# Half's turns one by one in slot 28, a written-out end with residuals added on TensorE

## The chip, the cores and the metric

The kernel runs on one core of a Trainium2 chip. The metric is the device time of one execution in microseconds, the median of several runs. The profile is one execution taken by the hardware profiler; its times count from the span's start.

## The reference, cut to what matters

A two-layer decoder over x of shape (8, 128, 512). The change touches the last two of its six blocks, cross-attention with grouped queries and a routed low-rank layer, each followed by residual and LayerNorm:

```python
q = (query @ Wq + bq).reshape(B, L, NKV, G, HDIM)          # 8 key heads x 4 queries x 128
k_, v_ = jnp.split(kv @ Wkv + bkv, 2, axis=-1)
scores = jnp.einsum('blkgd,bmkd->bkglm', q, k) * scale
attn = jax.nn.softmax(scores, axis=-1)
o = jnp.einsum('bkglm,bmkd->blkgd', attn, v).reshape(B, L, NHEAD * HDIM)
x = layernorm(x + o @ Wo + bo)

logits = jnp.einsum('bsd,ed->bse', x, route_w)             # 8 experts
topk_v, topk_idx = jax.lax.top_k(logits, 1)
route_weight = one_hot(topk_idx[..., 0], E) * topk_v
h = jnp.einsum('bsd,erd->bser', x, A)                      # rank 16
out = jnp.einsum('bser,eor->bso', route_weight[..., None] * h, Bw)
x = layernorm(x + out)
```

## The kernel before, in words

All engines have one straight program each, and meet by counting semaphores. The batch of 8 blocks of 128 tokens is worked in two halves of HB = 4 blocks. The attention is a chain of *slots*: slot s is key head `s // 4 % 8` with block `s % 4` of half `s // 32`; `v = s // HB` numbers head and half together. Slots 0 to 31 are the first half, 32 to 63 the second. float32 products are made of three products of split operands (`mm3`, L547 to L549: high with high, high with low, low with high); ScalarE writes the high part, and GpSimd (weights, L1407) or VectorE (activations) the rest.

In slot s TensorE does, in this order: the scores of slot s into bank 1 (L982); one query product of the next head into bank 0 (`query`, twelve products); the transposes of the probabilities of slot s-1 into bank 2 (L1001, `ident` from `prm`); the values weighed by the probabilities of s-2 into bank 3; and the output product of s-4, twelve products that accumulate over the eight heads in bank 4 + block. VectorE does `soft_a` (maximum L2040, subtraction L2043), `soft_b` (sum L2049, reciprocal, multiply L2053), `turned_rest_p` (L2059, the rest of the transposed probabilities of s-1) and `o_rest` (L2066, the rest of the output of s-2). ScalarE does the exponential, `query_out`, two high parts of weights (`split_q`, `split_o`), the high part of the transposed probabilities and of the values' output, and a value's high part. GpSimd does the rests of a query weight, an output weight and a value.

Slot 28 is the one in which the second half's tokens are first needed, transposed and split: `turn_half(1, i, bank)` makes four transposes of a block (L914, two records each), `turned_half` reads them on ScalarE into the high part of `xs` (`x_split`), `x_rest` (L2029) writes the rest. Before, all four blocks are turned between scores and query product, in banks 2 and 0 by turns:

```python
if s == (NKV - 1) * HB:
    for i in range(HB):
        if i == 0:
            pe.wait_ge(S.p_rest, s - 1)
        turn_half(1, i, (2, 0)[i % 2])
query(v + 1, b)
```

A block's LayerNorm after the attention (`ln_a(4, b)`, `ln_b(4, b)`): VectorE adds the bank to the token block in `x_tok`, to which GpSimd added the bias before (L1652), takes the statistics (L1654, L1655), adds epsilon (L1656); GpSimd raises it to -0.5 (`rstd`, L1391); VectorE subtracts and multiplies (L1660). Then follows the routed layer in four steps: four transposes of the block (L948), eight records of a product with `ra_sb`, 128 columns of A and 8 of logits (L957), the transpose of the weighed part `wh` (L962), and the product with `bw_sb` (L965, one float32 product, two records). Between, VectorE's `route(b)` copies the 8 logits out of PSUM (L2073), takes their maximum (MAX8, L2074), the index, a mask, and multiplies (L2080). Then comes a last LayerNorm, stage 5, and the store of the block from SyncE's queue.

For the first half these steps are put one per slot into slots 40 to 55 (`routed_at`, `ROUTED_FROM`). For the second half the loop runs on to 72 slots: the slots after 63 hold the last steps of the attention and a pipeline of the four routed steps. There VectorE works stage 4 of a block, then `route` of an earlier one, then `ln_a(5)` and `ln_b(5)` of one before that.

## Time and profile before

| What | us |
|---|---|
| median of 3 runs (lowest, highest) | 1334.72 (1332.58, 1335.19) |
| the profiled execution, its own time | 1333.96 |
| its span | 1332.2 |
| TensorE busy, share of the span | 1236.0, 93% |
| VectorE busy | 968.5, 73% |
| ScalarE busy | 748.2, 56% |
| GpSimd busy | 674.8, 51% |

The attention's slots run from about 811 to 1310, the rest is what comes before and the routed end. In the names of the profile PE is TensorE (PEld its weight loads), DVE VectorE, ACT ScalarE, POOL GpSimd, SP SyncE. All of ScalarE's instructions have the line L1035, that of a helper, so they are told by their tiles. The matmul records are pipelined: one's end lies after the next one's start. The idle time in brackets is that of the engine ahead of the instruction, with what ended it. PEclk is the clock that TensorE was granted, 1.00 for 2.4 GHz, 0.50 for 1.2 GHz.

### The profile page before, as it was taken

How to read it: one execution, taken by the hardware profiler on the slowest of the kernel's cores; microseconds unless marked ns; L12 is line 12 of the kernel's file. 1: busy time of each engine (PE TensorE's matmuls, PEld its weight loads, DVE VectorE, ACT ScalarE, POOL GpSimd, SP SyncE). 2: the span in 40 equal slices, each digit the busy share in tenths (PEclk: the TensorE clock that was granted, in tenths of full speed). 3: DMA queues.
4: the chain of work that ended last, by engine and by line, in shares of the span. 5: the costliest groups of instructions: out<-in, count | busy, mean ns of one | idle time of the engine just before them, and what ended most of it. 6: DMA issues, size and time to landing. Idle time of an engine off the chain costs nothing.

```text
span 1332.2 us, 18653 instructions
## 1 busy us (share of the span) xinstructions
PE 1236.0 (93%) x6464; PEld 925.4 (69%) x6464; DVE 968.5 (73%) x1770; ACT 748.2 (56%) x1478; POOL 674.8 (51%) x535
## 2 busy tenths in 40 slices
PE   6997899999998988998998999999998999999995
PEld 5876677767777764444565547888887888888874
DVE  4785798999999997898657766655554675666676
ACT  5479898989998983332133235544544445444441
POOL 4128988888988870222842126443433543333331
PEclk9999899999999999999999999999998999999999
DMA  6003200122220015002300103222221221111110
GB/s 182 12 26 139 75 25 25 35 93 88 88 72 1 1 56 136 16 9 85 144 9 16 40 24 103 80 73 71 68 75 48 80 79 65 63 64 64 48 48 32
DMA packets 37213, 81.92 MB, mean 61 GB/s; under 512 B 3808, under 2 KB 8160, under 8 KB 35200
## 3 DMA queue, kind: packets, MB, share of 16 engines
q1 hardware_dynamic: 37120, 80.72, 18.5%
q8 instruction: 53, 0.87, 0.3%
q14 instruction: 40, 0.33, 0.1%
HBM read 74.35 MB, written 6.36 MB: 61 GB/s over the span
## 4 chain that ended last, share of the span: by engine, by line
PE 68%; DVE 19%; ACT 6%; issue 5%; POOL 1%; DMA 1%; SPq 1%; DVEq 0%; POOLq 0%; ACTq 0%
PE psum L547 10%; PE psum L549 10%; PE psum L548 10%; PE psum L622 7%; PE psum L636 6%; PE psum L982 4%; DVE arena L1747 4%; PE psum L660 3%; PE psum L647 3%; ACT arena L1035 3%; PE psum L747 2%; PE psum L1001 2%; PE psum L731 1%; DVE lnst L1654 1%; PE psum L871 1%
## 5 line engine op out<-in xcount | busy, mean ns | idle before, releaser
L1471 POOL TENSOR_TENSOR arena<-arena 128x1024 f32<-128x1024 f32 x128 | 300.4, 2370 | 42.7 <-DVE arena L1747 42.5
L1407 POOL TENSOR_TENSOR w_split<-arena,w_split 128x512 fp32r<-128x512 f32 x128 | 168.1, 1333 | 280.3 <-ACT w_split L1035 280.3
L1747 DVE TENSOR_TENSOR_SCAN arena<-psum,arena 128x512 f32<-128x512 f32 x256 | 292.3, 1204 | 15.2 <-ACT psum L1035 15.2
L622 PEld LDWEIGHTS psum<-prm,arena 128*128 128x128 f32 x1024 | 118.7, 142 | 110.3 <-issue 61.8
L1035 ACT ACTIVATE psum<-arena,amat 128x508 f32<-128x508 f32 x256 | 173.3, 709 | 30.4 <-DVE arena L1747 29.4
L622 PE MATMUL psum<-prm,arena 128*128 128x128 f32 x1024 | 148.9, 280 | 38.4 <-DVE arena L1747 34.7
L1035 ACT ACTIVATE arena<-psum,ssmC 128x256 f32<-128x256 f32 x448 | 177.5, 484 | 10.8 <-PE psum L622 10.7
L1035 ACT ACTIVATE arena<-arena 128x512 f32<-128x512 f32 (+2 forms) x86 | 62.8, 734 | 210.1 <-DVE arena L2043 209.1
L1035 ACT ACTIVATE arena<-psum,prm 128x512 f32<-128x512 f32 (+1 forms) x130 | 91.1, 708 | 148.6 <-PE psum L549 70.0
L636 PE MATMUL psum<-prm,arena 128*128 128x128 f32 x1024 | 134.1, 273 | 0.1
L636 PEld LDWEIGHTS psum<-prm,arena 128*128 128x128 f32 x1024 | 117.0, 141 | 0.4 <-ACT arena L1035 0.3
L547 PE MATMUL psum<-x_split,w_split 128*128 128x512 f32 x256 | 106.3, 415 | 2.9 <-DVE x_split L2029 2.8
L1035 ACT ACTIVATE arena<-psum 128x512 f32<-128x512 f32 (+4 forms) x108 | 57.8, 563 | 82.7 <-PE psum L739 33.3
L1391 POOL TENSOR_TENSOR lnrs<-lnve,halfneg 128x1 f32<-128x1 f32 x48 | 28.4, 591 | 143.3 <-DVE lnve L1656 143.3
L549 PE MATMUL psum<-x_split,w_split 128*128 128x512 f32 x256 | 100.9, 394 | 0.0
L548 PE MATMUL psum<-x_split,w_split 128*128 128x512 f32 x256 | 100.8, 394 | 0.0
L547 PE MATMUL psum<-w_split,o_split 128*128 128x512 f32 x256 | 100.7, 394 | 0.0
L549 PE MATMUL psum<-w_split,o_split 128*128 128x512 f32 x256 | 100.1, 391 | 0.0
L548 PE MATMUL psum<-w_split,o_split 128*128 128x512 f32 x256 | 99.6, 389 | 0.0
L2040 DVE TENSOR_REDUCE amax<-psum 128x4 f32<-128x512 f32 x64 | 44.1, 688 | 52.4 <-PE psum L982 52.4
L2059 DVE TENSOR_TENSOR ssmT<-psum,p_split 128x512 fp32r<-128x512 f32 x64 | 44.2, 691 | 51.5 <-ACT p_split L1035 51.4
L2049 DVE TENSOR_REDUCE asum<-arena 128x4 f32<-128x512 f32 x64 | 43.9, 686 | 44.0 <-ACT arena L1035 44.0
(230 smaller groups left out, 2544.0 us busy)
## 6 DMA issues: line engine op xcount, KB each, us to landing
arena<-wq SPq DMA_DIRECT2D x64, 256.0 KB, 2.6
arena<-wo SPq DMA_DIRECT2D x64, 256.0 KB, 2.8
arena<-bc_scratch SPq DMA_DIRECT2D x8, 1024.0 KB, 5.2
arena<-win SPq DMA_DIRECT2D x16, 256.0 KB, 2.7
v_keep<-row SPq DMA_DIRECT2D x16, 256.0 KB, 2.1
arena<-v_keep SPq DMA_DIRECT2D x1, 4096.0 KB, 12.8
arena<-xT SPq DMA_DIRECT2D x8, 256.0 KB, 5.5
x_tok<-wv SPq DMA_DIRECT2D x1, 2048.0 KB, 7.7
```

What stands on the lines that cost most here:

```text
L547: mm(o, l[0], r[0], start=start, stop=False)
L548: mm(o, l[0], r[1], start=False, stop=False)
L549: return mm(o, l[1], r[0], start=False, stop=stop)
L622: last = nc.tensor.transpose(hT[:, c, b % 2, e, :], hst[:, (2 * k + e) % 4, b * L:(b + 1) * L], ident)
L636: last = mm(bank[6 + e][:, b * L:(b + 1) * L], hTs[:, k % 2, b, e, :], ident, start=(n == 0 and b == 0), stop=(n == NS - 1 and b == HB - 1 ...
L982: last = mm(bank[1][:, j * P:(j + 1) * P], qT[:, v % 2, j, b * L:(b + 1) * L], KT[:, v % NKV, gb * L:(gb + 1) * L], start=True, stop=True)
L1035: return nc.scalar.activation(o, i, f, **k)
L1407: gp.tensor_tensor(out_, whole, hi.bitcast(F32), ALU.subtract).then_inc(done, 1)
L1471: gp.tensor_tensor(bu[:, i % 4, :, :], dtu[:, (2 * j + e) % 4, :].unsqueeze(1).to_broadcast([P, NG, HT]), Brep[:, q * NG:(q + 1) * NG, :], ...
L1747: v.tensor_tensor_scan(hst[:, i % 4, :], decay_bank(i), bu[:, (k // NG * 2 + e) % 4, k % NG, :], 0.0, ALU.mult, ALU.add).then_inc(S.scan_d ...
L2040: link(v.tensor_reduce(amax[:, :], ps, AX.X, ALU.max))
L2059: v.tensor_tensor(p_lo[:, r % 2, :], bank[2][:, :], p_hi[:, r % 2, :].bitcast(F32), ALU.subtract).then_inc(S.p_rest, 1)
```

## The change

Four things. (1) In slot 28 the four blocks are turned one at a time through bank 0: the first after the scores, the other three between the four parts of the output product of slot 24; each waits until `x_rest` of the one before is done (`x4_lo`). The query product of the slot goes to the end, and on the other engines what belongs to it moves behind. (2) The loop ends with slot 63, and the end is written out: TensorE's last output products come one after the other with a single turn between them, the four routings stand in an order of their own with logits in banks 2 and 1 by turns. In slots 60 to 63 (`DRAIN`) ScalarE makes the transposed probabilities' high part ahead of the exponential and the output weight's high part late, and VectorE takes the probabilities' rest between the subtraction and the sum. (3) The residual of the second half is added by TensorE: after the output product of slots 56 to 59 it multiplies `ident` with the token block, in float32, into the same bank, so that stage 4's LayerNorm of these blocks reads PSUM and has no addition. Stage 5 of block 4 lies between the routings, the others behind them. (4) `route` searches the logits where they lie in PSUM, without the copy.

```diff
@@ tensor
             def turn_half(h, b, bk):
                 gb = h * HB + b
                 pe.wait_ge(S.x_done, lnc(3, gb))
-                if b >= 2:
+                if h and b:
+                    pe.wait_ge(S.x4_lo, gb)
+                elif b >= 2:
                     pe.wait_ge(S.x4_lo, gb - 1)
...
+            def logits_of(b):
+                pe.wait_ge(S.ra_in, 32)
+                pe.wait_ge(S.xT_sb, 2 * B + b + 1)
+                if b > HB:
+                    pe.wait_ge(S.r_wh, b - 1)
+                elif b >= 1:
+                    pe.wait_ge(S.r_wh, b)
+                for k in range(KD):
+                    last = mm(route_at(b), x5T[:, b % 2, k, :], ra_sb[:, k, :], start=(k == 0), stop=(k == KD - 1))
+                last.then_inc(S.r_ps, 1)
...
+            def attn_out(r):
+                rv, rb = r // HB, r % HB
+                pe.wait_ge(S.o_sb, r + 1)
+                if rv == NKV:
+                    pe.wait_ge(S.x_sum, lnc(4, rb))
+                for j in range(GQ):
+                    pe.wait_ge(S.wo_lo, rv * GQ + j + 1)
+                    last = mm3(bank[4 + rb][:, :], [osp[:, e, r % 3, j * P:(j + 1) * P] for e in range(2)],
+                               [wos[:, e, (rv * GQ + j) % 8, :] for e in range(2)],
+                               start=(rv % NKV == 0 and j == 0), stop=(rv % NKV == NKV - 1 and j == GQ - 1))
+                    if j == GQ - 1:
+                        last.then_inc(S.op_ps, 1)
+                    elif r == TURNING - 4:
+                        turn_half(1, j + 1, 0)
+                if rv == NU - 2:
+                    pe.wait_ge(S.xbias, 2 * B + HB + rb + 1)
+                    mm(bank[4 + rb][:, :], ident, x_tok[:, HB + rb, :], start=False, stop=False)
...
-                    if s == (NKV - 1) * HB:
-
-                        for i in range(HB):
-                            if i == 0:
-                                pe.wait_ge(S.p_rest, s - 1)
-                            turn_half(1, i, (2, 0)[i % 2])
-                    query(v + 1, b)
+                    if s == TURNING:
+                        turn_half(1, 0, 0)
+                    else:
+                        query(v + 1, b)
+                if s >= 1:
+                    turn_probs(s)
+                if s >= 2:
+                    weigh_values(s - 2)
+                if s >= 4:
+                    attn_out(s - 4)
+                if s == TURNING:
+                    query(v + 1, b)
...
+            turn_probs(SLOTS)
+            weigh_values(SLOTS - 2)
+            attn_out(SLOTS - 4)
+            weigh_values(SLOTS - 1)
+            attn_out(SLOTS - 3)
+            attn_out(SLOTS - 2)
+            turn_routed(HB, 0)
+            attn_out(SLOTS - 1)
+            pe.wait_ge(S.p_rest, SLOTS)
+            logits_of(HB)
+            turn_routed(HB + 1, 3)
+            turn_routed(HB + 2, 0)
+            logits_of(HB + 1)
+            turn_wh(HB, 3)
+            routed_out(HB, 4)
+            pe.wait_ge(S.xT_sb, 2 * B + HB + 3)
+            turn_routed(HB + 3, 0)
+            logits_of(HB + 2)
+            turn_wh(HB + 1, 3)
+            logits_of(HB + 3)
+            routed_out(HB + 1, 5)
+            turn_wh(HB + 2, 3)
+            routed_out(HB + 2, 6)
+            turn_wh(HB + 3, 3)
+            routed_out(HB + 3, 7)
@@ scalar
+                if s >= DRAIN:
+                    probs_high(s - 1)
+                act.wait_ge(S.p_es, s + 1)
+                av(pe_[:, s % 2, :], pe_[:, s % 2, :], ACT.Exp, scale=SQ).then_inc(S.p_exp, 1)
+                if s == TURNING:
+                    turned_half(1, 0, 0)
+                    probs_high(s - 1)
+                    turned_half(1, 1, 0)
+                    outs_high(s - 2)
+                    turned_half(1, 2, 0)
+                    split_o(s)
+                    turned_half(1, 3, 0)
+                elif s < DRAIN:
                     query_out(v + 1, b)
...
+                if s >= DRAIN:
+                    split_o(s)
                 value_high(s)
+                if s == TURNING:
+                    query_out(v + 1, b)
+                    split_q((v + 1) * GQ + b + 3)
@@ gpsimd
-                    rest_q(s + 7)
+                    if s != TURNING:
+                        rest_q(s + 7)
...
+                    if s == TURNING:
+                        rest_q(s + 7)
...
+            for stage in (4, 5):
+                for b in range(HB, B):
+                    rstd(pool, stage, b)
@@ vector
-                link(v.tensor_copy(logits, bank[2][:, P:P + 8]))
-                link(v.max(rt8, logits))
-                link(v.max_index(ri8[:, :], rt8, logits))
+                link(v.max(rt8, route_at(b)[:, P:P + 8]))
+                link(v.max_index(ri8[:, :], rt8, route_at(b)[:, P:P + 8]))
...
+            def attn_ln_a(b):
+
+                dve.wait_ge(S.op_ps, NU * HB - B + b + 1)
+                link(v.bn_stats(lnst[:, b, :], bank[b][:, :]))
+                link(v.bn_aggr(lnmv[:, b, :], lnst[:, b, :]))
+                v.tensor_scalar(lnve[:, b:b + 1], lnmv[:, b, 1:2], 1e-5, None, ALU.add).then_inc(S.ln_ve, 1)
...
+                soft_a(s)
+                if s == TURNING:
+                    x_rest(1, 0, 0)
                     turned_rest_p(s - 1)
+                    x_rest(1, 1, 0)
                     o_rest(s - 2)
+                    x_rest(1, 2, 0)
+                    x_rest(1, 3, 0)
+                if s >= DRAIN:
+                    turned_rest_p(s - 1)
+                soft_b(s)
...
+            turned_rest_p(SLOTS - 1)
+            o_rest(SLOTS - 2)
+            attn_ln_a(HB)
+            o_rest(SLOTS - 1)
+            attn_ln_b(HB)
+            for b in range(HB + 1, B):
+                attn_ln_a(b)
+                attn_ln_b(b)
+            route(HB)
+            route(HB + 1)
+            routed_ln_a(HB)
+            route(HB + 2)
+            ln_b(5, HB)
+            route(HB + 3)
+            for b in range(HB + 1, B):
+                routed_ln_a(b)
+                if b > HB + 1:
+                    ln_b(5, b - 1)
+            ln_b(5, B - 1)
```

## Rows read from the trace of the kernel before

**Rows 1.** Busy by stretch: length; PE, PEld, DVE, ACT, POOL; PEclk, DMA share, GB/s.

```profile
1003.15:1010.65 7.50, 7.50 (x41) 6.35 (x41) 4.29 (x7) 3.62 (x7) 2.94 (x4) 1.00 0.23 71
1010.65:1027.00 16.35, 12.34 (x57) 9.84 (x57) 6.87 (x11) 5.79 (x11) 2.97 (x4) 0.79 0.10 31
1018.00:1022.50 4.50, 4.50 (x11) 3.53 (x12) 0.66 (x2) 0.00 (x0) 0.00 (x0) 0.50 0.00 0
1312.00:1320.00 8.00, 4.42 (x27) 2.77 (x26) 6.15 (x24) 1.52 (x4) 1.10 (x2) 1.00 0.09 33
```

**Rows 2.** Timeline of slot 28: start, length, engine, line, tiles; idle time before it.

```profile
1010.49 1.05 PE L982 MATMUL psum<-arena 128*128 128x128 f32 x8
...
1011.37 1.04 PE L914 MATMUL psum<-prm,x_tok 128*128 128x128 f32 x8
...
1013.56 1.06 ACT L1035 ACTIVATE x_split<-psum 128x512 fp32r<-128x512 f32 x2
...
1014.17 1.29 DVE L2029 TENSOR_TENSOR x_split<-psum,x_split 128x512 fp32r<-128x512 f32 x2 [1.18 <-ACT x_split L1035]
...
1015.01 1.53 PE L914 MATMUL psum<-prm,x_tok 128*128 128x128 f32 x8 [2.60 <-DVE x_split L2029]
...
1017.95 0.80 PE L547 MATMUL psum<-x_split,w_split 128*128 128x512 f32 x1 [1.41 <-DVE x_split L2029]
```

**Rows 3.** Timeline of slots 62 and 63, VectorE and GpSimd.

```profile
1285.94 0.69 DVE L2049 TENSOR_REDUCE asum<-arena 128x4 f32<-128x512 f32 x1 [0.70 <-ACT arena L1035]
...
1286.51 1.29 POOL L1407 TENSOR_TENSOR w_split<-arena,w_split 128x512 fp32r<-128x512 f32 x1 [3.53 <-ACT w_split L1035]
...
1286.88 1.47 DVE L2053 TENSOR_TENSOR arena<-arena,ainv 128x512 f32<-128x512 f32 x1
...
1292.56 1.47 DVE L2053 TENSOR_TENSOR arena<-arena,ainv 128x512 f32<-128x512 f32 x1
```

**Rows 4.** TensorE's timeline from slot 60 to its last attention product.

```profile
1271.37 1.05 PE L982 MATMUL psum<-arena 128*128 128x128 f32 x8
...
1276.14 1.05 PE L982 MATMUL psum<-arena 128*128 128x128 f32 x8
...
1294.78 0.63 PE L1001 MATMUL psum<-prm,arena 128*128 128x128 f32 x4 [1.35 <-DVE ssmT L2059]
...
1302.94 0.63 PE L948 MATMUL psum<-prm,x_tok 128*128 128x128 f32 x4 [0.39 <-DVE o_split L2066]
...
1306.18 1.09 PE L957 MATMUL psum<-arena 128*128 128x136 f32 x8
...
1307.46 0.48 PE L547 MATMUL psum<-w_split,o_split 128*128 128x512 f32 x1
...
1310.08 0.39 PE L549 MATMUL psum<-w_split,o_split 128*128 128x512 f32 x1
```

**Rows 5.** The last blocks: timelines of VectorE and TensorE.

```profile
1322.57 0.17 DVE L2074 MAX8 arena<-arena 128x8 f32<-128x8 f32 x1
...
1323.58 0.29 DVE L2080 TENSOR_TENSOR arena<-psum,arena 128x128 f32<-128x128 f32 x1
...
1323.79 0.68 DVE L1652 TENSOR_TENSOR x_tok<-x_tok,psum 128x512 f32<-128x512 f32 x1
...
1324.62 1.12 PE L965 MATMUL psum<-arena 128*128 128x512 f32 x2 [0.37 <-ACT arena L1035]
...
1325.45 0.15 DVE L1656 TENSOR_SCALAR lnve<-lnmv 128x1 f32<-128x1 f32 x1
...
1326.27 0.55 DVE L1660 TENSOR_SCALAR x_tok<-x_tok,lnmv,lnrs 128x512 f32<-128x512 f32 x1 [0.66 <-POOL lnrs L1391]
...
1329.20 0.55 DVE L1660 TENSOR_SCALAR x_tok<-x_tok,lnmv,lnrs 128x512 f32<-128x512 f32 x1 [0.66 <-POOL lnrs L1391]
```

**Rows 6.** Chain of waits, slot 43: start, length, engine, tile, line.

```profile
1141.47 0.87 PE psum L965 x2
```

**Rows 7.** GpSimd's timeline, earlier network stage: a power beside VectorE's second half.

```profile
789.28 0.77 POOL L1391 TENSOR_TENSOR lnrs<-lnve,halfneg 128x1 f32<-128x1 f32 x1 [1.41 <-DVE lnve L1656]
```

More of the change, by code:

```diff
@@ L421, in routed_at, with route_at @@
                 return [(at // 4, at % 4, 2)]
-            at = s - (2 * NKV * HB + 1)
-            return [(HB + at - k, k, ((at % 2), 2, 3, 4 + at - k)[k]) for k in (3, 2, 1, 0) if 0 <= at - k < HB]
-        SLOTS = 2 * NKV * HB + 8
+            return []
+        def route_at(b):
+            return bank[1 if b > HB and b % 2 else 2][:, 0:136]
+        SLOTS = 2 * NKV * HB
+        DRAIN = SLOTS - HB
         @block.sync
@@ new lines, in turn_routed @@
+            def turn_routed(b, bk):
+                pe.wait_ge(S.x_done, lnc(4, b))
+                if b >= 2:
+                    pe.wait_ge(S.xT_sb, 2 * B + b - 1)
+                for k in range(KD):
+                    last = nc.tensor.transpose(bank[bk][:, k * P:(k + 1) * P], x_tok[:, b, k * P:(k + 1) * P], ident)
+                last.then_inc(S.xTt, 1)
+            def logits_of(b):
[5 more added lines that the diff above has]
+                    pe.wait_ge(S.r_wh, b)
+                for k in range(KD):
+                    last = mm(route_at(b), x5T[:, b % 2, k, :], ra_sb[:, k, :], start=(k == 0), stop=(k == KD - 1))
+                last.then_inc(S.r_ps, 1)
@@ new lines, in turn_wh, with routed_out, turn_probs @@
+            def turn_wh(b, bk):
+                pe.wait_ge(S.r_wh, b + 1)
+                if b > HB:
+                    pe.wait_ge(S.whT_done, b)
+                nc.tensor.transpose(bank[bk][:, 0:P], wh, ident).then_inc(S.wh_ps, 1)
+            def routed_out(b, bk):
+                pe.wait_ge(S.whT_done, b + 1)
+                mm(bank[bk][:, :], whT, bw_sb, start=True, stop=True).then_inc(S.rf_ps, 1)
+            def turn_probs(s):
+                pe.wait_ge(S.p_norm, s)
+                if s >= 2:
+                    pe.wait_ge(S.p_rest, s - 1)
+                for rb, step, bk in routed_at(s - 1):
+                    pe.wait_ge((S.xT_sb, S.r_wh, S.whT_done, S.x_sum)[step],
+                               (2 * B + rb + 1, rb + 1, rb + 1, lnc(5, rb))[step])
+                for j in range(GQ):
+                    last = nc.tensor.transpose(bank[2][:, j * P:(j + 1) * P], pn[:, j * P:(j + 1) * P], ident)
+                last.then_inc(S.t_ps, 1)
@@ new lines, in _ @@
+                if s >= 2:
+                    weigh_values(s - 2)
+                if s >= 4:
+                    attn_out(s - 4)
+                if s == TURNING:
+                    query(v + 1, b)
+                for rb, step, bk in routed_at(s):
+                    pe.wait_ge(S.p_rest, s)
+                    if step == 0:
+                        turn_routed(rb, bk)
+                    elif step == 1:
+                        logits_of(rb)
+                    elif step == 2:
+                        turn_wh(rb, bk)
+                    else:
+                        routed_out(rb, bk)
```

185 lines of the change are left out of this document (71 added, 114 removed).

## The prediction

> **What bounds the kernel now.** I read the busy time by stretch first, then the timelines of three places that the diff touches, one engine at a time, and last the chain of waits over the end. In a plain slot of the attention TensorE is busy for all of 7.50 us at the full clock, with VectorE at 4.29 and ScalarE at 3.62 [rows 1]. So whatever the change does for VectorE in slots 0 to 59 is free, and worth nothing, unless TensorE waits for it. Three places are different.
>
> *Slot 28* lasts 16.35 us, from 1010.65 to 1027.00 [rows 1], 8.85 more than a plain one. Four batches of transposes belong in it; eight of them (two batches) take 1.04 [rows 2], so four batches are some 1.8 us of work. The rest is waiting and clock. After the first two batches TensorE stands idle for 2.60, after the next two for 1.41 [rows 2]: both banks are full, and ScalarE and VectorE empty them only after the slot's maximum, subtraction and exponential. After the idle 2.60 the granted clock is 0.50 (1.2 GHz) until about 1022.5 [rows 1].
>
> *Slots 60 to 63* have no query products left, and VectorE sets their length: in the chain of waits its normalising multiply comes back every 5.68 us, at 1286.88 and 1292.56 [rows 3]. TensorE alone needs only 4.77 for such a slot (1271.37 to 1276.14, without a wait) [rows 4]. VectorE loses 0.70 per slot waiting for the exponential, and its multiply takes 1.47, because GpSimd's subtraction started at 1286.51 and ended at 1287.80, 0.9 after the multiply began [rows 3].
>
> *The end.* TensorE finishes the last attention product at 1310.08+0.39 = 1310.47 [rows 4]; call that moment V. From V to the end of the last normalisation, 1329.20+0.55 = 1329.75 [rows 5], VectorE has almost all the work, with a wait for GpSimd's power in each LayerNorm.
>
> **The change, part by part.**
>
> *Slot 28.* The batches now go through bank 0 one at a time, with other work between, and the query product goes last. I lay it out on the old times. Scores as before; batch 0 follows, done about 1012.0. TensorE goes on with the probabilities' transposes, the value product and the first of the four output products, to about 1013.7: work that before came behind the queries. ScalarE reads batch 0 at 1013.56 as before, VectorE has its rest from 1014.17 on, and the next batch starts at 1015.01, as it did [rows 2]: stall 1.3. From there each round is: 0.6 until the transposes are visible, 0.6 on ScalarE, 0.7 on VectorE, 0.15 to restart, some 2.1 (1015.0, 1017.1, 1019.2, 1021.3), with 0.45 of transposes and 0.7 of output product inside, so a stall of 0.9 to 1.0 each. The query product starts at 1021.3 rather than at 1017.95 [rows 2]. But it then runs in 2.8 at full clock, where before it took 5 us and left 4.2 of other work behind it; slot 29 starts at 1024.1 instead of 1027.0: 2.9 us saved. GpSimd's rest of the next query weight now comes last in its slot, after the query product (visible at 1024.3) and two ScalarE copies, at about 1025.6, inside slot 29; that weight is for slot 31, and the load that it releases in SyncE's queue (with the output weight queued behind) is needed from slot 30 on: hidden.
>
> *Clock in slot 28.* That sum wants the clock kept. The old fall stands behind 4.35 us in which TensorE was busy 1.76, one gap of 2.60. The new slot has no gap over 1.3. From 1312 to 1320 TensorE is busy only 4.42 of 8 us, broken up by waits, and the granted clock is 1.00 [rows 1]; the new slot from 1011.4 to 1021.3 is busy about 5.8 of 9.9, the same share. I take the full clock, and keep a low one as a rival.
> The Trainium skill, "TensorE: Matmul & The Clock Gate", PE-mode transpose, says that transposes don't count as activity for the clock; by that rule the new stretch is poorer than its busy share says, the clock falls, and the slot gains next to nothing (the second case below). No row here separates transposes from products.
>
> *Slots 60 to 63.* VectorE takes the probabilities' rest during the exponential, so 0.6 of its 5.68 goes, and GpSimd's subtraction comes later in the slot, so the multiply may be back near 0.7. VectorE needs 4.2 to 5.0. But TensorE gets a float32 identity product of 128x512 per slot, which takes 0.87 (two records) [rows 6]: 4.77+0.87 = 5.64. TensorE becomes the bound at practically the old period. Four slots from 1271.37 give 1293.9 for the transposes of slot 64, with switching and VectorE's last multiply 1294.1, against 1294.78 [rows 4]: 0.7 saved. Bounds for the identity product: 0.6 if part is hidden, and 1.12, as the last such product reads [rows 5], which would cost 1.0 over four slots.
>
> *From slot 64 to V.* Before, 15.69 (1294.78 to 1310.47). Out of it go the first logits and one batch of transposes, now issued after V (1306.18 to 1307.46, 1.28 [rows 4]), and the wait before 1302.94 (0.39 shown, 0.54 with the restart), because the awaited LayerNorm ends near 1301.2 without its addition. The rest stays: 13.9. V comes at 1308.0: 2.5 earlier in all.
>
> *From V on.* Before 19.28. A LayerNorm's first half is 1.81 (addition to the end of the epsilon, 1323.79 to 1325.60); its addition is 0.72 of that (0.68 and the hand-over); its second half starts 0.67 after, and takes 0.55; a routing without its copy takes 1.30 (MAX8 at 1322.57 to 1323.87); from there the transposed weight, ScalarE's copy and the output product need 1.87 (to 1325.74) [rows 5]. VectorE's instructions that need no result of the last one start 0.08 early. The attention LayerNorms of the other three blocks end before V (the third near V-0.9). The new order: last attention LayerNorm 0.04+1.09+0.67+0.68 (it reads PSUM; 0.68 is what the addition that reads PSUM takes), routing 4 1.22, gives V+3.70; routing 5 hides behind the 1.87, and the first half of output 4 ends at V+3.70+1.87+0.04+1.81 = V+7.42. Routing 6, second half 4, routing 7: 1.22+0.46+1.22, V+10.32. First halves 5 and 6, second half 5, first half 7: 1.72+1.73+0.47+1.72, V+15.96. The last power is issued just as VectorE runs a second half, and there GpSimd's power reads 0.77 instead of 0.55 [rows 7], so 0.89 rather than 0.67, then 0.55: V+17.40. Saved: 1.9.
> GpSimd's delay is what the Trainium skill, "SBUF — State Buffer", Who interferes with whom, describes as a port held for a whole instruction; by it the last multiply of slot 63 could go either way, 0.3 for the sum. The 0.77 agrees.
> If reading PSUM cost `max` and the index search more, they have no row here; a reduction over 512 columns of SBUF takes 0.69 and an addition that reads as many of PSUM 0.68 [rows 3, 5], so I take nothing, with 0.4 as the bound. The same copy in slots 41, 45, 49 and 53 lies beside a full TensorE: 0.
>
> *The last store* starts when its block is done; before that took 1332.2-1329.75 = 2.45. Now three blocks finish within 3.2 us and their transfers may overlap: +0.2 (bounds 0 and 1.2).
>
> **Sum.** -2.9 -0.7 -1.8 -1.9 +0.2 = -7.1. The profiled execution took 1333.96 (span 1332.2), so 1326.9. The median of the runs is 0.76 above that execution; I add half: 1327.3. What can't be told from no change is about 0.2%, 2.7 us.
>
> **The rivals.**
> 1. *Forecast*, 1325.0 to 1328.8 by the bounds: chance 0.62.
> 2. *The clock falls in slot 28 all the same*, because the new slot is broken up four times. At 0.50 a product is issued every 0.43 instead of 0.23; twelve of the query lose 2.4. Gain of the slot 0.3, time 1329.9. For it: a busy share under 0.6 for 10 us, in the slot where the clock fell before; against: the full clock at 1312 to 1320. Chance 0.20.
> 3. *The end gives less*: identity products at 1.12 and transfers at their bound, or an order in which VectorE waits for ScalarE's copy, which now waits for TensorE's transposes of the same slot. 1.0+1.0 less: 1329.3 to 1330. For it: VectorE's queue in slots 60 to 63 is strung to TensorE's twice. Against: a margin of 0.7 to 1.4 per slot. Chance 0.09.
> 4. *Nothing gained*: slot 28 ends no earlier and slots 60 to 63 are as in 3, within 2.7 of before. Chance 0.05.
> 5. *Slower*: the clock falls early in slot 28 and stays through the next slots, as products of 0.43 stretch them. A us at the low clock costs about 0.47 of a full TensorE. To eat the 4.2 of the end and pass 0.2% it must cost 6.9 more than the old fall did (about 2.7: eleven products at 0.2 more, and eight transposes in 1.53 instead of 1.04): some 20 us low instead of 7.4. Time 1337.5 or more. Against: at 1018 to 1022.5 TensorE was full at the low clock and got the high one back. Chance 0.04.
>
> Range for 8 in 10: 1324.4 to 1330.6, case 1 and 2 and most of 3. Chances: faster by over 0.2% 0.91, within 0.05, slower 0.04.
>
> **What will show it.** Slot 28 from scores to scores 13.4 instead of 16.35, four batches 2.1 apart, granted clock 1.00; slots 60 to 63 with TensorE never idle and 5.64 apart; identity products at 0.87; V at 1305.1 in the new trace (1308.0 less slot 28's 2.9), 17.4 from V to the last normalisation. Wrong would be: products of 0.43 in slot 28's query, an idle TensorE before the probabilities' transposes in slots 61 to 64, or a last store that lands over 3 us after its block.

## The result, and the profile after

The median falls from 1334.72 to 1328.37 us (7 runs each, 1326.71 to 1333.13 after, 1332.58 to 1337.17 before), a ratio of 0.995 with a 95% interval of 0.9932 to 0.9968. 1327.3 was predicted, 1324.4 to 1330.6 as the range.

The two profiled executions say less at first sight: spans of 1331.3 and 1332.2. To read them I cut each span at starts of slots, the scores' first record on TensorE. "Head" is all before slot 0; V is the end of the last attention product, as in the prediction.

| Stretch, us | before | after | difference | predicted |
|---|---|---|---|---|
| head, code unchanged | 811.40 | 817.80 | +6.40 | 0 |
| slot 28 | 16.35 | 13.72 | -2.63 | -2.9 |
| slot 29 | 7.50 | 7.72 | +0.22 | 0 |
| slots 30 to 59 | 237.03 | 237.04 | 0 | 0 |
| slot 60 to the transposes of slot 64 | 23.41 | 22.58 | -0.83 | -0.7 |
| from there to V | 15.69 | 13.40 | -2.29 | -1.8 |
| V to the last normalisation's end | 19.28 | 17.56 | -1.72 | -1.9 |
| last store | 2.45 | 2.38 | -0.07 | +0.2 |
| all but the head | | | -7.32 | -7.1 |

The spans are given to 0.1 us, so the last store and all sums to the end of the span are known to about 0.1.

The head is the same code in both. It was longer here because the clock was lower at places in it: over the whole head it is 0.98 in after and 0.99 in before, and over the fourteen profiled executions of this document the longest head, 822.41, has the lowest clock, 0.97. These are the windows of busy time of after, then of before, at two of those places (length; busy PE, PEld, DVE, ACT, POOL; granted clock, DMA share, GB/s):

```profile
469.00:500.00 31.00, 28.92 (x185) 22.53 (x184) 26.52 (x29) 26.01 (x57) 22.03 (x11) 0.94 0.08 22
800.00:806.00 6.00, 5.99 (x18) 4.11 (x18) 5.02 (x13) 1.21 (x2) 0.89 (x2) 0.72 0.00 0
```

```profile
469.00:500.00 31.00, 27.86 (x186) 21.48 (x187) 28.08 (x30) 26.53 (x58) 20.95 (x11) 1.00 0.18 65
800.00:806.00 6.00, 5.99 (x24) 4.07 (x23) 3.20 (x9) 1.53 (x3) 2.85 (x4) 1.00 0.21 66
```

The windows lie at the same distance from the start; after is some us behind in its work by 800. There its TensorE is full and works at 0.72 of its clock, where before's has 1.00. Which execution meets this is chance: the spans of after's seven runs go from 1324.9 to 1331.3, and the profiled one is the longest. 1332.2 less 7.32 is 1324.9, the shortest of them.

Slot 28 of after, as windows of busy time (the slot, and the stretch from the second turn to the query product) and as TensorE's timeline with the copy of the query product on ScalarE (start, length, engine, line, tiles; idle time before it), to hold against [rows 1, 2]:

```profile
1016.90:1030.62 13.72, 10.19 (x57) 7.71 (x55) 6.87 (x11) 4.68 (x9) 2.29 (x4) 1.00 0.12 37
1021.43:1027.74 6.31, 3.98 (x21) 2.61 (x22) 3.24 (x6) 3.08 (x6) 1.72 (x2) 1.00 0.00 0
```

```profile
1016.90 1.05 PE L1029 MATMUL psum<-arena 128*128 128x128 f32 x8
...
1017.79 0.60 PE L921 MATMUL psum<-prm,x_tok 128*128 128x128 f32 x4
...
1021.43 0.63 PE L921 MATMUL psum<-prm,x_tok 128*128 128x128 f32 x4 [1.21 <-DVE x_split L2110]
...
1023.57 0.63 PE L921 MATMUL psum<-prm,x_tok 128*128 128x128 f32 x4 [0.81 <-DVE x_split L2110]
...
1025.70 0.63 PE L921 MATMUL psum<-prm,x_tok 128*128 128x128 f32 x4 [0.80 <-DVE x_split L2110]
...
1027.74 0.50 PE L552 MATMUL psum<-x_split,w_split 128*128 128x512 f32 x1 [0.71 <-DVE x_split L2110]
...
1030.62 1.05 PE L1029 MATMUL psum<-arena 128*128 128x128 f32 x8
...
1030.82 0.69 ACT L1084 ACTIVATE arena<-psum,prm 128x512 f32<-128x512 f32 x1 [3.66 <-PE psum L554]
...
1031.65 0.47 PE L552 MATMUL psum<-x_split,w_split 128*128 128x512 f32 x1
```

The turns (L921) stand 2.14 and 2.13 apart, each behind VectorE's rest of the block before, with TensorE idle 1.21, 0.81, 0.80 and 0.71. The granted clock is 1.00 over the whole slot, where [rows 1] have 0.79. The last two rows show what the prediction took for free: the copy of the query product begins at 1030.82, after the scores of slot 29, and the next query product needs the bank it empties: it starts 1.03 after the scores (1030.62 to 1031.65). Where ScalarE is not in the way it starts 0.81 after (slot 30: 1038.34 to 1039.15). Each turn is four records, one for each transpose, and not two for each as the description of the kernel has it.

Slots 60 to 63 of after, from the timelines of TensorE, VectorE and GpSimd; here L1013 is the product with the identity:

```profile
1275.38 1.05 PE L1029 MATMUL psum<-arena 128*128 128x128 f32 x8
...
1281.02 1.05 PE L1029 MATMUL psum<-arena 128*128 128x128 f32 x8
...
1279.53 0.69 DVE L2134 TENSOR_TENSOR arena<-arena,ainv 128x512 f32<-128x512 f32 x1
...
1279.73 1.62 POOL L1483 TENSOR_TENSOR w_split<-arena,w_split 128x512 fp32r<-128x512 f32 x1 [5.02 <-ACT w_split L1084]
...
1297.10 1.02 PE L1013 MATMUL psum<-x_tok,prm 128*128 128x512 f32 x2
...
1297.96 0.60 PE L986 MATMUL psum<-prm,arena 128*128 128x128 f32 x4
```

Slots are 5.64 apart (1275.38 to 1281.02), and an identity product occupies TensorE for 0.86 (1297.10 to 1297.96). VectorE's multiply is back at 0.69, since it starts 0.20 ahead of GpSimd's subtraction; now that takes 1.62 instead of 1.29 [rows 3].

The end of after, the same three timelines (L965 the logits; L2166, L2172 the attention's LayerNorm; MAX8 the beginnings of routings 4 and 5; L2178 the addition of output 4; L1467, L1741 the last power and what it releases), beside [rows 5]:

```profile
1311.20 1.09 PE L965 MATMUL psum<-arena 128*128 128x136 f32 x8
...
1311.40 0.70 DVE L2166 BATCH_NORM_STATS2 lnst<-psum 128x6 f32<-128x512 f32 x1 [0.63 <-PE psum L554]
...
1313.17 0.81 DVE L2172 TENSOR_SCALAR x_tok<-psum,lnmv,lnrs 128x512 f32<-128x512 f32 x1 [0.66 <-POOL lnrs L1467]
...
1313.90 0.17 DVE L2154 MAX8 arena<-psum 128x8 f32<-128x8 f32 x1
...
1315.12 0.17 DVE L2154 MAX8 arena<-psum 128x8 f32<-128x8 f32 x1
...
1317.12 0.69 DVE L2178 TENSOR_TENSOR x_tok<-x_tok,psum 128x512 f32<-128x512 f32 x1 [0.70 <-PE psum L976]
...
1327.55 0.78 POOL L1467 TENSOR_TENSOR lnrs<-lnve,halfneg 128x1 f32<-128x1 f32 x1 [1.41 <-DVE lnve L2181]
...
1328.37 0.55 DVE L1741 TENSOR_SCALAR x_tok<-x_tok,lnmv,lnrs 128x512 f32<-128x512 f32 x1 [0.44 <-POOL lnrs L1467]
```

V is at 1311.36; the last normalisation ends at 1328.37+0.55 = 1328.92.

### The profile page after: what moved, and what is told of

It is laid out like the page before. It is cut to its first block, busy times and chain, and to the rows that moved or that the text cites. A ratio compares the mean times of both kernels' runs of the same rounds, so it can differ in the third digit from the quotient of the medians.

```text
span 1331.3 us, 18656 instructions
## 1 busy us (share of the span) xinstructions
PE 1241.9 (93%) x6472; PEld 929.3 (70%) x6472; DVE 963.0 (72%) x1758; ACT 748.9 (56%) x1478; POOL 674.2 (51%) x535
## 4 chain that ended last, share of the span: by engine, by line
PE 70%; DVE 17%; ACT 6%; issue 4%; POOL 1%; DMA 1%; SPq 1%; DVEq 0%; POOLq 0%; ACTq 0%
PE psum L552 10%; PE psum L554 10%; PE psum L553 10%; PE psum L627 7%; PE psum L641 6%; PE psum L1029 4%; DVE arena L1828 4%; PE psum L665 4%; PE psum L652 3%; ACT arena L1084 3%; PE psum L752 2%; PE psum L986 2%; PE psum L736 1%; PE psum L876 1%; PE psum L647 1%
## 5 line engine op out<-in xcount | busy, mean ns | idle before, releaser
L1467 POOL TENSOR_TENSOR lnrs<-lnve,halfneg 128x1 f32<-128x1 f32 x48 | 28.8, 600 | 139.5 <-DVE lnve L1737 114.7
L1084 ACT ACTIVATE w_split<-arena 128x512 fp32r<-128x512 f32 (+1 forms) x129 | 74.8, 624 | 0.0
```

Source lines behind the costliest of these rows:

```text
L1084: return nc.scalar.activation(o, i, f, **k)
```

## The experiments

Twelve kernels ran. All readings of stretches are from each one's profiled execution; "60 to end" is from the scores of slot 60 to the end of the span.

| Kernel | head | 28 + 29 | 30 to 59 | slots 60, 61, 62 | 60 to end |
|---|---|---|---|---|---|
| before | 811.40 | 23.85 | 237.03 | 4.77, 5.76, 5.68 | 60.83 |
| after | 817.80 | 21.44 | 237.04 | 5.64, 5.65, 5.65 | 55.92 |
| turns_only | 811.58 | 21.44 | 237.03 | 4.78, 5.74, 5.70 | 60.75 |
| end_only | 815.27 | 23.84 | 237.09 | 5.64, 5.65, 5.64 | 55.99 |
| turns_in_a_row | 811.24 | 24.24 | 237.02 | 5.64, 5.65, 5.65 | 55.98 |
| copy_back | 812.02 | 21.47 | 237.03 | 5.64, 5.64, 5.65 | 56.57 |
| old_drain | 812.00 | 21.42 | 237.01 | 5.64, 5.74, 5.68 | 57.07 |
| no_identity | 813.03 | 21.40 | 236.98 | 4.77, 4.78, 4.77 | 53.39 |
| fill | 813.46 | 17.55 | 237.31 | 5.64, 5.65, 5.64 | 55.96 |
| early | 812.36 | 21.42 | 237.01 | 5.65, 5.64, 5.65 | 55.51 |
| early_mended | 812.15 | 21.41 | 236.98 | 5.65, 5.64, 5.65 | 54.86 |
| fill_no_identity | 822.41 | 17.56 | 237.32 | 4.77, 4.78, 4.77 | 53.40 |
| fill_noid_early | 813.71 | 17.55 | 237.29 | 4.77, 4.77, 4.78 | 52.16 |
| fill_noid_unmended | 811.38 | 17.56 | 237.29 | 4.77, 4.77, 4.78 | 52.26 |

Stretches with the same code repeat within 0.1, the head within 11. So differences under 3 us are judged by stretches, and ratios of whole times carry the large ones only. Each ratio in this section is to runs of the kernel before of its own (medians from 1335.60 to 1339.09), and is not a quotient of medians.

### The two halves of the change, each alone

turns_only is the kernel before with the new slot 28; end_only is the changed kernel with the old one. The cut is ScalarE's part of end_only:

```diff
-                if s == TURNING:
-                    turned_half(1, 0, 0)
-                    probs_high(s - 1)
-                    turned_half(1, 1, 0)
...
+                if s == TURNING:
+                    for i in range(HB):
+                        turned_half(1, i, (2, 0)[i % 2])
...
```

> The kernel before with slot 28 alone as in the changed one (one turn at a time through bank 0, query product last). If the parts are independent: slots 28 and 29 take 21.4 us together (before 23.85), the stretch from the scores of slot 60 to the end of the span stays at 60.8, and the time falls by 2.4. Rival: part of the changed kernel's gain in slot 28 is a clock that happened to stay up, and here it falls: slot 28 at 15 to 16 with a granted clock of 0.8, gain under 1.

> The changed kernel with slot 28 as before: the end, the residuals on TensorE and the search in PSUM alone. If the parts are independent: slot 28 back at 16.35 us, from the scores of slot 60 to the end of the span 55.9 (before 60.8), time 4.9 below before. Rival: the end depends on what slot 28 leaves (a clock, a queue of loads), then the last stretch differs by more than 0.3 from 55.9.

turns_only: 21.44 for slots 28 and 29 and 60.75 for the end, so 2.41 in the one place and nothing in the other. As a whole time it can't be told from no change: 1335.07, ratio 0.9992 (0.9963 to 1.0021). end_only: 23.84 and 55.99; 1330.89, ratio 0.9956 (0.9931 to 0.9981). The halves add up to after's 7.32 within 0.1: there is no interplay.

### The clock: the turns in a row

All turns ahead of the output product, so that nothing but transposes stands between the waits.

```diff
-                    elif r == TURNING - 4:
-                        turn_half(1, j + 1, 0)
...
+                if s == TURNING:
+                    for i in range(1, HB):
+                        turn_half(1, i, 0)
                 if s >= 4:
                     attn_out(s - 4)
```

> The changed kernel with turns 1 to 3 of slot 28 all ahead of the output product, so TensorE has nothing between them and is idle for some 2.7, 1.7, 1.7 and 1.7 us. If idle time on TensorE is what brought the clock down in the old slot: granted clock 0.5 for the output and query products, slot 28 at 17 to 19.5 us. If it is not: full clock, slot 28 at 14.8, just 1.1 above the changed kernel's 13.7.

Busy time of this kernel by windows: the whole slot, the stretch with the second and third turn, and what follows.

```profile
1010.30:1026.80 16.50, 11.60 (x56) 9.35 (x56) 6.86 (x11) 4.69 (x9) 2.36 (x4) 0.79 0.09 31
1014.50:1018.00 3.50, 1.62 (x8) 1.13 (x8) 2.18 (x4) 1.18 (x2) 0.00 (x0) 0.65 0.00 0
1018.00:1022.00 4.00, 2.50 (x9) 2.14 (x9) 1.34 (x3) 1.91 (x4) 1.68 (x2) 0.50 0.00 0
```

TensorE's timeline of the three late turns:

```profile
1014.88 0.63 PE L921 MATMUL psum<-prm,x_tok 128*128 128x128 f32 x4 [1.90 <-DVE x_split L2111]
...
1017.01 1.08 PE L921 MATMUL psum<-prm,x_tok 128*128 128x128 f32 x4 [1.50 <-DVE x_split L2111]
...
1019.60 1.08 PE L921 MATMUL psum<-prm,x_tok 128*128 128x128 f32 x4 [1.50 <-DVE x_split L2111]
```

The slot is as long as before's: 16.50 (one run: 1329.35), with a clock of 0.79 like [rows 1]. With the idle times at 1.90, 1.50 and 1.50, the clock falls to 0.50 (1.2 GHz), and the batches of transposes at 1017.01 and 1019.60 take 1.08 instead of 0.63. It recovers while the output products run (0.96 from 1022 to 1027). So the theory of the clock had the fall right and its cost too high: 16.50 instead of 17 to 19.5, where 14.8 was expected at the full clock. By that 14.8, an estimate, some 1.7 of the slot is the clock's and 1.1 idle time. What it shows is that work between the turns, not the single bank, makes the slot shorter: same number of waits, same data.

In after TensorE is busy 3.98 of 6.31 between its turns at full clock; here 1.62 of 3.50 with a falling one. The Trainium skill, "TensorE: Matmul & The Clock Gate", PE-mode transpose, has it that transposes don't count as activity. By that rule some 1.2 of the 3.98 drop out in after (three turns, each 0.38 until the next product starts), and its clock stayed at 1.00 all the same. Neither run separates transposes from idle time as the cause of the fall: in turns_in_a_row more idle time and a stretch of nothing but transposes came together.

### The end: identity products, copy, order of the last slots

no_identity lets VectorE add the residual of blocks 4 to 7 again and read the sum from SBUF, the statistics and the second half (`attn_ln_b`) alike:

```diff
-                if rv == NU - 2:
-                    pe.wait_ge(S.xbias, 2 * B + HB + rb + 1)
-                    mm(bank[4 + rb][:, :], ident, x_tok[:, HB + rb, :], start=False, stop=False)
...
-                link(v.bn_stats(lnst[:, b, :], bank[b][:, :]))
+                dve.wait_ge(S.xbias, 2 * B + b + 1)
+                link(v.tensor_tensor(x_tok[:, b, :], x_tok[:, b, :], bank[b][:, :], ALU.add))
+                link(v.bn_stats(lnst[:, b, :], x_tok[:, b, :]))
...
```

> The changed kernel without the four identity products; VectorE adds the residual at the start of the last four attention LayerNorms, as before. Theory: TensorE sets slots 60 to 63 only because of these products (0.87 each); without them a slot takes 4.8 to 5.1 instead of 5.65, the last LayerNorm behind the attention costs 0.72 more at its start and 0.26 less at its end, and the last stretch falls from 55.9 to between 53.0 and 54.0: the residual on TensorE is a loss. Rival: VectorE or the chain through ScalarE holds a slot at 5.6 even so, and the stretch grows to 56.4: the residual on TensorE is a small gain.

It is faster than after: 53.39 instead of 55.92, and 1325.8, ratio to before 0.9899 (0.9858 to 0.9939). TensorE's and VectorE's timelines:

```profile
1270.51 1.05 PE L1026 MATMUL psum<-arena 128*128 128x128 f32 x8
...
1275.28 1.05 PE L1026 MATMUL psum<-arena 128*128 128x128 f32 x8
...
1289.72 0.66 PE L986 MATMUL psum<-prm,arena 128*128 128x128 f32 x4
...
1303.07 0.55 DVE L2171 TENSOR_SCALAR x_tok<-x_tok,lnmv,lnrs 128x512 f32<-128x512 f32 x1 [0.66 <-POOL lnrs L1464]
...
1303.55 0.69 DVE L2164 TENSOR_TENSOR x_tok<-x_tok,psum 128x512 f32<-128x512 f32 x1
```

Slots are 4.77 apart, as long as TensorE's work without the identity, and the transposes of slot 64 come 19.21 after slot 60 rather than 22.58: 3.37 for four products, 0.84 each. That is 0.03 less than the slots differ by (5.64 to 4.77), because without them TensorE waits 0.1 for VectorE before these transposes. Of the 3.37, 0.39 are lost at the value product behind them (it starts 0.75 after the transposes, in after 0.36), and 0.45 after V, where the addition of block 7 costs 0.72 and the second half, from SBUF again, takes 0.55 instead of 0.81. Blocks 4 to 6 have their additions beside a full TensorE; block 7's comes at 1303.55, 0.04 after V (1303.51), as VectorE is just through with block 6.

copy_back restores the copy of the logits, old_drain the old order of ScalarE and VectorE in slots 60 to 63:

```diff
-                link(v.max(rt8, route_at(b)[:, P:P + 8]))
-                link(v.max_index(ri8[:, :], rt8, route_at(b)[:, P:P + 8]))
+                link(v.tensor_copy(logits, route_at(b)[:, P:P + 8]))
+                link(v.max(rt8, logits))
+                link(v.max_index(ri8[:, :], rt8, logits))
```

```diff
-                if s >= DRAIN:
-                    turned_rest_p(s - 1)
                 soft_b(s)
-                if 1 <= s < DRAIN and s != TURNING:
+                if 1 <= s and s != TURNING:
                     turned_rest_p(s - 1)
```

> The changed kernel with the copy of the logits out of PSUM put back in all eight routings. Theory: 0.19 us in each routing of VectorE's last stretch, of which the second is partly hidden behind the wait for the first output product: 0.6 to 0.8 more from the scores of slot 60 to the end (55.9 to 56.5 or 56.7), and nothing in slots 40 to 55, which stay at their lengths within 0.05. Rival: reading PSUM made maximum and search slower by as much, and nothing changes.

> The changed kernel with the old order of ScalarE and VectorE in slots 60 to 63 (exponential ahead of the probabilities' high part, output weight early, probabilities' rest behind the multiply). Theory: the slots stay near 5.65 since TensorE sets them with the identity product, VectorE's 5.69 is level with that, GpSimd's subtraction blocks the multiply again (1.47), and the transposes of slot 64 come 0.6 to 0.8 later. Rival: two engines level at 5.7 wait for each other in turn, slots of 6.3 or more, 2 us lost. Other rival: order makes no difference, 0.

copy_back (one run, 1327.94) costs 0.65 at the end by the table, and 0.57 up to the end of the last normalisation, which is read to 0.01: the lower edge of what was expected. It costs nothing in the first half's routings: from slot 40 to slot 56 every kernel of the table takes 131.55 to 131.61, with the copy or without. old_drain (1328.76) costs 1.15, more than expected. GpSimd's, VectorE's and TensorE's timelines of it:

```profile
1284.68 1.29 POOL L1480 TENSOR_TENSOR w_split<-arena,w_split 128x512 fp32r<-128x512 f32 x1 [3.55 <-ACT w_split L1084]
...
1285.05 1.47 DVE L2131 TENSOR_TENSOR arena<-arena,ainv 128x512 f32<-128x512 f32 x1
...
1292.95 0.63 PE L986 MATMUL psum<-prm,arena 128*128 128x128 f32 x4 [0.47 <-DVE ssmT L2137]
```

The old picture is back: the multiply starts 0.37 after GpSimd's subtraction and takes 1.47, slots 61 and 62 go at 5.74 and 5.68 (before: 5.76 and 5.68), and TensorE waits before the transposes of slot 64, 23.42 after slot 60 (before: 23.41). So beside identity products the new order is worth 0.84 before slot 64 and 0.3 behind it. Four kernels now give that stretch with and without each of the two: neither 23.41 (before), identity products alone 23.42 (old_drain), both 22.58 (after), the new order alone 19.21 (no_identity). Without identity products the order is worth 4.20.

### What was still left: slot 28's idle time

fill takes the output product of slot 25 into slot 28 too, between the turns, and the scores of slot 29 ahead of the query product. In the cut, `{2: 1}` means that behind part 2 of this output product comes the turn of block 1:

```diff
+                if s == TURNING:
+                    scores(s)
+                    turn_half(1, 0, 0)
+                    turn_probs(s)
+                    weigh_values(s - 2)
+                    attn_out(s - 4, {2: 1})
+                    attn_out(s - 3, {0: 2, 2: 3})
+                    scores(s + 1)
+                    query(v + 1, b)
+                elif s == TURNING + 1:
+                    turn_probs(s)
+                    weigh_values(s - 2)
+                    query(v + 1, b)
...
```

> The changed kernel with slot 29's scores and output product (of slot 25) moved into slot 28's stalls between the turns, and in slot 29 the probabilities' transposes and the value product ahead of the query product. TensorE's stalls of 1.21, 0.81, 0.80 and 0.71 and slot 29's extra 0.22 leave 3.8 us to fill with 3.64 of work: slots 28 and 29 together 17.8 to 18.5 instead of 21.4, time about 3 below the changed kernel. Rival: VectorE or ScalarE, now needed for slot 29 sooner, pass the wait on to slots 29 to 31, which then lose what slot 28 gains.

A window over both slots of this kernel, and TensorE's timeline with the scores of slots 28, 29 and 30 and the first query product of slot 30:

```profile
1012.50:1030.00 17.50, 17.24 (x96) 14.10 (x95) 9.87 (x17) 6.42 (x12) 4.64 (x6) 1.00 0.09 31
```

```profile
1012.58 1.05 PE L1028 MATMUL psum<-arena 128*128 128x128 f32 x8
...
1022.54 1.05 PE L1028 MATMUL psum<-arena 128*128 128x128 f32 x8
...
1030.13 1.05 PE L1028 MATMUL psum<-arena 128*128 128x128 f32 x8
...
1031.16 0.47 PE L552 MATMUL psum<-x_split,w_split 128*128 128x512 f32 x1
```

TensorE is busy 17.24 of 17.50. Slots 28 and 29 take 17.55 instead of 21.44, below the 17.8 to 18.5 expected; slots 30 to 59 give 0.27 back. It is slot 30 that gives it back, 7.76 instead of 7.51: its query product starts 1.03 after its scores (1030.13 to 1031.16), as that of slot 29 does in after. The hold-up by ScalarE's copy has moved one slot on, which is the rival in small, and the 3.62 that is left is the 3.64 of work that was moved. Time: 1326.27, ratio 0.9908 (0.9882 to 0.9935).

### The end once more: an earlier start of the routings

early issues the transposes and the logits of block 4 ahead of the last output product, and the transpose of its weighed part inside it, so that its routing and output are done sooner. On VectorE the first routing and the first half of output 4 move in among the last attention LayerNorms:

```diff
+                    if r == SLOTS - 1 and j == 2:
+                        turn_wh(HB, 0)
...
-            attn_out(SLOTS - 2)
             turn_routed(HB, 0)
-            attn_out(SLOTS - 1)
+            attn_out(SLOTS - 2)
             pe.wait_ge(S.p_rest, SLOTS)
             logits_of(HB)
+            pe.wait_ge(S.o_sb, SLOTS)
             turn_routed(HB + 1, 3)
+            attn_out(SLOTS - 1)
+            logits_of(HB + 1)
+            routed_out(HB, 4)
             turn_routed(HB + 2, 0)
-            logits_of(HB + 1)
...
+            attn_ln_a(HB + 2)
             route(HB)
+            attn_ln_b(HB + 2)
+            attn_ln_a(HB + 3)
+            routed_ln_a(HB)
+            attn_ln_b(HB + 3)
             route(HB + 1)
-            routed_ln_a(HB)
...
```

> The changed kernel with the first routing moved ahead of the last output product: block 4's turn before the output product of slot 62, its logits before that of 63, its weighed part turned inside it, and on VectorE the first routing and the first half of its last LayerNorm inside the waits of the attention LayerNorms. TensorE ends the attention 1.2 later, VectorE saves one routing (1.22), the wait for the first output product (0.7) and one wait for the power (0.66): from the scores of slot 60 to the end 54.0 to 54.5 instead of 55.9. Rival: the order was bound by the transposes and copies of blocks 6 and 7, and nothing is won or something lost.

This missed: 55.51 instead of 55.92, only 0.41 (1328.66, ratio 0.9946, 0.9919 to 0.9973). TensorE's and VectorE's timelines:

```profile
1307.25 1.09 PE L965 MATMUL psum<-arena 128*128 128x136 f32 x8
...
1308.18 1.02 PE L976 MATMUL psum<-arena 128*128 128x512 f32 x2
...
1307.45 0.70 DVE L2167 BATCH_NORM_STATS2 lnst<-psum 128x6 f32<-128x512 f32 x1 [1.21 <-PE psum L554]
...
1309.23 0.69 DVE L2179 TENSOR_TENSOR x_tok<-x_tok,psum 128x512 f32<-128x512 f32 x1 [0.68 <-PE psum L976]
```

VectorE waits 1.21 for the last output product, which now ends 1.5 later after slot 60, and then 0.68 for output 4, which TensorE started only at 1308.18, behind the logits of block 5. The work taken out of VectorE's queue became two waits for TensorE. early_mended swaps just these two:

```diff
             attn_out(SLOTS - 1)
-            logits_of(HB + 1)
             routed_out(HB, 4)
+            logits_of(HB + 1)
```

> The early end of the run early, with identity products, and only the routed output of block 4 put ahead of the logits of block 5. If its place behind those logits was what held VectorE up, the wait before the addition of output 4 (0.68) and what follows from it go, and from slot 60 to the end comes to 54.2 to 55.0 against 55.51. If the late start of the last output product is what counts (that first wait, 1.21, is before output 4), it stays within 0.2 of 55.5.

```profile
1307.00 1.02 PE L976 MATMUL psum<-arena 128*128 128x512 f32 x2
...
1307.85 1.09 PE L965 MATMUL psum<-arena 128*128 128x136 f32 x8
...
1307.20 0.70 DVE L2167 BATCH_NORM_STATS2 lnst<-psum 128x6 f32<-128x512 f32 x1 [1.21 <-PE psum L554]
```

54.86 (one run: 1326.37): the second wait is gone (the addition follows at 1308.22), the first stays at 1.21, and 0.65 is won. So the order costs 0.65. The 0.36 above the upper edge of what was expected of early, 54.5, is about what V comes later than thought: 1.54 after slot 60 instead of 1.2.

### All together

fill_no_identity joins fill and no_identity; fill_noid_early adds the mended early end, and fill_noid_unmended has the routed output behind the logits again.

> The output product of slot 25 between the turns (as in fill), and the residual of blocks 4 to 7 added by VectorE again (as in no_identity). If the two gains stand in different places and each was read rightly, they add: slots 28 and 29 together 17.55, slots 30 to 59 237.3, slots 60 to 62 at 4.77, from slot 60's scores to the end 53.4, in all 308.2 after the scores of slot 28 against 321.7 of the kernel before: 13.5 less, a ratio of about 0.990. Rival: the residuals wait for something that only the slower slots of the changed kernel gave time for; then slots 60 to 63 stay at 4.77 but the end from the last attention product on is over 18.2.

> The same with the early end, mended where it waited: turn and weighed part of block 4 ahead of the last output product, and its routed output directly behind it, before the logits of block 5. If what cost the early end its gain was that output 4 stood behind logits 5, VectorE now works without a wait of over 0.4 from the last attention product on, and from slot 60 to the end 52.0 to 52.9, against 53.4 without it. If VectorE, which has the additions again, is late already when the last attention product ends, the order gives nothing or up to 0.5 back: 53.2 to 53.9.

> The run fill_noid_early (52.16 from slot 60 to the end) with the routed output of block 4 behind the logits of block 5 again. If that place costs what is thought, 52.8 to 53.4; if it costs nothing here because VectorE is still at block 7's statistics, 52.2. Together with the run before, it parts the order's share from that of the identity products: without identity products and with the order unmended the end would be 0.4 better than 53.4 if the shares add.

The gains add: 17.56 and 53.40. Its median says less than its stretches (1327.49 in 6 runs, ratio 0.9901, 0.9865 to 0.9938); its profiled execution had the longest head of all, 822.41. The early end takes the stretch from slot 60 on to 52.16: 1324.51, ratio 0.9897 (0.9852 to 0.9942). Without the mending it is 52.26, so the place of the routed output, worth 0.65 with identity products, is worth at most 0.10 here, no more than the spans are read to. So the output's place, which was the reason for the order of early_mended, isn't what makes the early end pay here, although the 52.16 lies where that reason put it. VectorE's timeline of fill_noid_early shows why:

```profile
1302.22 0.69 DVE L2177 TENSOR_TENSOR x_tok<-x_tok,psum 128x512 f32<-128x512 f32 x1 [0.75 <-PE psum L554]
...
1303.95 0.68 DVE L2190 TENSOR_TENSOR x_tok<-x_tok,psum 128x512 f32<-128x512 f32 x1
```

VectorE adds block 7 from 1302.22 on, and comes to output 4 at 1303.95; TensorE had started that product at 1302.02, 1.02 long. It is VectorE's own work, the addition among it, that now fills the time in which it had waited. By the stretches, fill_noid_early is 321.71 - 307.00 = 14.7 us faster than before from slot 28 on (after: 7.3), the most of the fourteen together with fill_noid_unmended. As whole times, fill, no_identity and the joined kernels (ratios of 0.9897 to 0.9908) can't be told apart; the single run of fill_noid_unmended took 1319.35.

## Why the prediction was right

The mechanism and the sum held: of the -7.1, -7.32 was measured in the stretches behind the head, and the terms were off by 0.5 at most, in both directions. That the median came within 1.1 of the forecast says less. The head alone differs by up to 11 us between executions, and the medians fell by 6.35, not by 7.32.

- **Slot 28, -2.9, measured -2.63, and +0.22 in slot 29.** The rounds of 2.1 and the stalls of 0.9 to 1.0 were 2.13 and 0.71 to 0.81. The slot is 0.3 longer than the 13.4 predicted, and half of that is a reading. The prediction lays the new slot out from the scores at 1010.49 [rows 2] and takes 1027.0, the end of a window that starts at 1010.65, for the next scores. These start 16.35 after 1010.49, at 1026.84, so its own layout, to 1024.1, saves 2.7 and not 2.9. In slot 29 the prediction looked for what comes late only on GpSimd and in SyncE's queue: the copy of the late query product on ScalarE holds up the query of slot 29.
- **The clock.** It stayed at 1.00, as the forecast had it. The rival was a real one: in turns_in_a_row the clock falls in the same slot with the same turns, and the slot then gains nothing. It did not cost 2.4 by slow products of the query, as the rival had it, but by idle time, two batches of transposes and the first four output products at the low clock. (By the rival's own numbers its gain would have been 2.9 less 2.4, 0.5 and not 0.3.)
- **Slots 60 to 63, -0.7, measured -0.83.** "TensorE becomes the bound at practically the old period" is what the slots 5.64 apart say. What the prediction did not ask is what the change is worth without this term: the identity products cost 3.37 at slot 64 and give back 0.84, a net loss of 2.5 which no_identity shows. Without them the slots up to 64 would have come down by 4.20 (23.41 to 19.21): VectorE's and ScalarE's new order made that room, and the identity products took 3.37 of it.
- **Slot 64 to V, -1.8, measured -2.29.** Out of it went the 1.28 and the 0.54 that were named, and a wait that was not seen: in before the value product starts 0.66 after the transposes of slot 64, in after 0.36. Of the rest, 0.17, some 0.1 is that in before one more output product follows a turn, which makes it 2.85 long (1303.33 to 1306.18) instead of 2.7.
- **V to the last normalisation, -1.9, measured -1.72.** The steps came as laid out: routings of 1.22, output 4's addition at V+5.76 (5.61 by the steps), the last power at 0.78 (0.77 was predicted from [rows 7]), 17.56 against 17.40. One size was wrong: the second half that reads PSUM takes 0.81, not 0.68. Searching PSUM costs what searching SBUF does (MAX8 0.17 in both).
- **Last store, +0.2, measured -0.07**, which is no difference at the 0.1 to which spans are read. Three blocks that end within 3.2 us do not hold up the last store.
- **The median.** The 0.4 added for the median's place above the profiled run was a guess about the head; it is far inside the spread of after's seven runs, 6 us. The median is nearer to the forecast than that spread lets one count on, which is luck.

Of the other rivals, that the end gives less (identity products at 1.12) is out: they take 0.86, and the slots follow each other at 5.64 to 5.65, the 4.77 of TensorE's work and one such product. With it go the rivals that nothing is gained or time is lost.

## What to carry to other kernels

Moving a piece of work from one engine to another is worth only what the engine it leaves was late by: cost the slot once with and once without the moved piece, since a reordering in the same change may have made room already. Independent work put between dependent turns pays twice, by the idle time it fills and by the clock it keeps, and the same holds at the end of a chain only if what is pulled forward doesn't push back the instruction that the other engine waits for next. Compare traces by stretches between the same landmarks when unchanged code varies by more than the change does.

## What the runs showed of the hardware

- VectorE and GpSimd delay each other, and the one that starts second pays. GpSimd 0.37 ahead: VectorE's multiply 1.47, the subtraction 1.29 (old_drain). VectorE 0.20 ahead: multiply 0.69, subtraction 1.62 (after). The Trainium skill, "SBUF — State Buffer", Who interferes with whom, has it that the order of issue decides which of the two blocks, and these rows agree with it. It calls the shared ports an exclusive lock; here the second loses a little less than the other's rest: 0.78 of 0.92, and 0.33 of 0.49.
- A subtraction and multiplication, each with one scalar per row, takes 0.55 from SBUF and 0.81 from PSUM; an addition of a PSUM tile to one of SBUF takes 0.69, and statistics of PSUM 0.70 against 0.69.
- The same code in the head took 811.24 to 822.41 in fourteen profiled executions, through stretches at a lower granted clock (0.72 with TensorE full, at 800 in after). The mean clock over the head is 0.97 in the longest, 0.99 in the shortest.
- The clock fell to 0.50 (1.2 GHz) behind an idle 1.90, in a stretch with TensorE busy 1.62 of 3.50 (turns_in_a_row), and not with 3.98 busy in 6.31 and no idle time over 1.21 (after).
